# A state-space layer and a linear-attention layer on one core: softplus of dt as one ScalarE table function, first conv taps on ScalarE, and a new order ahead of the scan

## What is computed

```python
xs = clamp(layernorm(groupnorm(x)))                 # 1024 x 256
xin, z = split(xs @ in_proj_w.T)                    # 512 channels each
xc = silu(causal_conv1d(xin, conv_w, 4 taps) + conv_b)
dt, Bm, Cm = split(xc @ x_proj_w.T)                 # 16 + 16 + 16
dt = softplus(dt @ dt_proj_w.T + dt_proj_b)         # 512 channels
h[t] = exp(dt[t] * A) * h[t-1] + dt[t] * xc[t] * B[t]   # 512 x 16 states
y = (h . C + xc * D) * silu(z)
out = clamp(layernorm(clamp(y @ out_proj_w.T)))
```

## Time and profile before

| | us |
|---|---|
| median of 3 runs | 708.2 (707.07 to 708.25) |
| profiled execution, its own time from first to last instruction | 709.2 |
| PE busy | 647.0 (91%) |
| DVE busy | 549.3 (77%) |
| ACT busy | 410.7 (58%) |
| POOL busy | 386.0 (54%) |

### The profile page before, as it was taken

The page is one execution under the profiler, slowest core; times in us unless marked ns, Lnnn a source line. Parts: engine busy times, 40 slices in busy tenths (PEclk is TensorE's granted clock), DMA queues, the critical chain, the costliest instruction groups (busy, mean ns, idle before and its releaser), DMA issues.

```text
span 709.2 us, 25428 instructions
## 1 busy us (share of the span) xinstructions
PE 647.0 (91%) x11476; PEld 450.7 (64%) x11476; DVE 549.3 (77%) x478; ACT 410.7 (58%) x810; POOL 386.0 (54%) x140
## 2 busy tenths in 40 slices
PE   3989986989989999889999999999898999999997
PEld 1434342679978899777898889854345555565532
DVE  5896758488978999799889989863769787892345
ACT  0765789898776777677778767502246346324100
POOL 1000346689996898789889998863101143533000
PEclk9999989999999999999999999999999999999999
DMA  7990352410084201522340100016039899760202
GB/s 213 77 72 4 84 158 114 116 42 18 20 183 90 59 23 24 146 63 63 100 116 18 48 19 18 4 33 184 0 84 199 174 244 228 167 115 2 55 3 119
DMA packets 72627, 62.12 MB, mean 88 GB/s; under 512 B 34024, under 2 KB 57576, under 8 KB 72520
## 3 DMA queue, kind: packets, MB, share of 16 engines
q1 hardware_dynamic: 71560, 60.09, 38.5%
q10 hardware_dynamic: 960, 0.41, 0.2%
HBM read 44.22 MB, written 15.25 MB: 84 GB/s over the span
## 4 chain that ended last, share of the span: by engine, by line
PE 68%; POOL 11%; ACT 9%; DVE 6%; issue 5%; DMA 1%; POOLq 0%; DVEq 0%; ACTq 0%
PE PS L1237 23%; PE PS L1356 8%; PE PS L1470 6%; PE PS L1259 5%; POOL X L572 5%; PE PS L1119 5%; PE PS L1454 4%; POOL arena L572 3%; POOL WIN L572 3%; PE PS L1285 2%; PE PS L1374 2%; PE PS L1256 2%; DVE X L1734 1%; PE PS L1070 1%; PE PS L1335 1%
## 5 line engine op out<-in xcount | busy, mean ns | idle before, releaser
L572 POOL TENSOR_TENSOR X<-X,spare 128x2048 f32<-128x2048 f32 x32 | 146.7, 4584 | 19.2 <-ACT mid L860 9.4
L1237 PE MATMUL PS<-mid,arena 128*32 128x128 f32 x4096 | 138.6, 275 | 9.3 <-issue 8.0
L1237 PEld LDWEIGHTS PS<-mid,arena 128*32 128x32 f32 x4096 | 124.1, 111 | 20.4 <-issue 14.2
L1237 PE MATMUL PS<-WPR,arena 128*32 128x128 f32 x2048 | 130.3, 273 | 4.6 <-issue 1.9
L1237 PE MATMUL PS<-APROD,arena 128*32 128x128 f32 x2048 | 129.5, 273 | 2.9 <-issue 2.9
L1237 PEld LDWEIGHTS PS<-WPR,arena 128*32 128x32 f32 x2048 | 112.1, 110 | 16.0 <-issue 8.9
L1237 PEld LDWEIGHTS PS<-APROD,arena 128*32 128x32 f32 x2048 | 110.7, 110 | 4.7 <-issue 4.1
L852 ACT ACTIVATE arena<-arena,small 128x512 f32<-128x512 f32 (+1 forms) x150 | 99.4, 711 | 22.0 <-DVE X L1734 11.7
L572 POOL TENSOR_TENSOR WIN<-WIN,spare 128x2048 f32<-128x2048 f32 x16 | 73.3, 4584 | 13.3 <-DVE WIN L1734 10.3
L597 POOL TENSOR_TENSOR arena<-arena,PWR 128x512 f32<-128x512 f32 x30 | 42.7, 1450 | 69.3 <-PE PS L1356 69.2
L572 POOL TENSOR_TENSOR arena<-arena,spare 128x2048 f32<-128x2048 f32 x16 | 73.2, 4575 | 9.2 <-DVE arena L1734 5.9
(11 more groups left out here) (203 smaller groups left out, 1192.1 us busy)
## 6 DMA issues: line engine op xcount, KB each, us to landing
arena<-dt_rows SPq DMA_DIRECT2D x56, 256.0 KB, 4.2
arena<-patch_rows SPq DMA_DIRECT2D x40, 324.0 KB, 6.1
patch_rows<-arena SPq DMA_DIRECT2D x10, 648.0 KB, 7.4
X<-in_x SPq DMA_DIRECT2D x4, 1024.0 KB, 7.4
dt_rows<-arena SPq DMA_DIRECT2D x8, 512.0 KB, 2.6
spare<-c_rows SPq DMA_DIRECT2D x64, 64.0 KB, 2.1
tap_rows<-WPR SPq DMA_DIRECT2D x24, 88.0 KB, 8.7
mid<-dt_rows SPq DMA_DIRECT2D x8, 256.0 KB, 3.9
```

Source lines behind the costliest of these rows:

```text
L572: pool.tensor_tensor(HB[s % 4], HB[s % 4], CROW[:, k % 2:k % 2 + 1, :].broadcast_to([P, QN, HALF]), ALU.mult).then_inc(S["g_rd"], 1)
L1237: mm = pe.matmul(PS[32 * n:32 * n + 32, 4 + i, j * P:(j + 1) * P], DXT[:, DT_ * b + g, 4 * h + j, 32 * i:32 * i + 32], DIAGB[k % 2][n][:, ...
```

## The change

Softplus becomes one ACT instruction from PSUM to dt; the passes on DVE and POOL go, and DVE takes the largest dt by a reduction of its own (`largest_dt`). All eight first taps are on ACT. The copies of z pieces 4 and 5 go. The lists of ACT, PE, DVE, POOL and SP and the pairs are written in a new order. The scan no longer waits for corrections (`sp_corr`, `sp_sum`).

```diff
-        PAIR_USERS = ("x3 z0 x6 x7 xd1 V4 V7 tr4 tr6 y0".split(),
-                      "x2 x5 V1 tr0 tr1 V5 tr2 tr3 tr5 tr7 halves0 y1".split(),
-                      "x1 xd0 z1 z2 z3 V3 V6 z7 u0".split(),
-                      "x0 x4 V0 V2 z4 z5 rates0 z6 u1".split())
+        PAIR_USERS = ("z0 x6 V3 z2 z4 z6 V6 tr4 tr6 y0".split(),
+                      "x2 xd0 z1 tr3 rates0 z7 V7 tr5 tr7 halves0 y1".split(),
+                      "x0 x3 x5 V1 tr0 x7 z3 z5 V4 u0".split(),
+                      "x1 x4 V0 V2 tr1 tr2 xd1 V5 u1".split())
-        FIRST_BY_SCALAR = (0, 1, 2)
-        COPIED = (4, 5)
...
@@ SP @@
             first_dt(1)
+            store_dt(2)
+            store_dt(3)
             store_c(1)
-            for e in range(2, NG):
+            for e in range(DT_, NG):
                 store_dt(e)
...
@@ POOL @@
-            def correct(e):
-                pool.wait_ge(S["sp_ln"], e + 1)
-                pool.wait_ge(S["um1_rd"], e + 1)
-                pool.tensor_tensor(LNB[:, e % 2], LNB[:, e % 2], UM1[e % 2], ALU.subtract).then_inc(S["sp_corr"], 1)
...
+            for e in range(NG):
+                times_x(e)
...
@@ ACT @@
-            def positive(e):
+            def softplus(e):
                 act.wait_ge(S["v_ps"], e + 1)
-                act.activation(dt(e), tile_pair("V", e), ACT.Relu).then_inc(S["sp_relu"], 1)
...
+                act.activation(dt(e), tile_pair("V", e), ACT.Softplus).then_inc(S["dt_rd"], 1)
...
-            half_way(4)
-            half_way(5)
+            half_way(0)
             decay(0)
-            take_dxt(3)
+            decay(1)
+            half_way(1)
             take_dxt(4)
+            for e in range(2, 6):
+                half_way(e)
+            take_dxt(5)
+            decay(2)
...
@@ PE @@
             project_in("x", 3)
+            project_in("z", 0)
+            project_in("x", 4)
             pe.wait_ge(S["ld_xp"], 32)
             xdbl(0, 0)
             xdbl(0, 1)
-            project_in("x", 4)
+            xdbl(0, 2)
             project_in("x", 5)
-            xdbl(0, 2)
             xdbl(0, 3)
-            project_in("z", 0)
             b_by_time(0)
+            project_in("x", 6)
             pe.wait_ge(S["ld_dtw"], 64)
             dt_preact(0)
-            project_in("x", 6)
             dt_preact(1)
             project_in("z", 1)
+            dt_preact(2)
+            dx_by_time(0)
+            dt_preact(3)
+            dx_by_time(1)
             project_in("x", 7)
             project_in("z", 2)
-            dt_preact(2)
+            dx_by_time(2)
             project_in("z", 3)
+            dx_by_time(3)
+            project_in("z", 4)
             xdbl(1, 0)
...
+            project_in("z", 5)
+            rates_by_four()
             xdbl(1, 3)
+            project_in("z", 6)
             b_by_time(1)
...
@@ DVE @@
+            def largest_dt(e):
+                dve.wait_ge(S["dt_rd"], e + 1)
+                dve.tensor_reduce(DTMAX[:, e:e + 1], dt(e), mybir.AxisListType.X, ALU.max).then_inc(S["top_rd"], 1)
...
             convolve(6)
-            rounded(0)
...
+            for e in range(DT_):
+                largest_dt(e)
+            rates(0)
             convolve(7)
...
+            for e in range(DT_, NG):
+                largest_dt(e)
             rates(1)
```

More of the change, by code:

```diff
@@ L326, in tile_pair @@
             return pair(pair_of(what, i))
-        def conv_partials(e):
-            return sum(KC - 2 if k in FIRST_BY_SCALAR else KC - 1 for k in range(e))
         def step_of(s):
@@ L694, in silu_gate @@
             def silu_gate(e):
-                if e in COPIED:
-                    act.wait_ge(S["zc_rd"], COPIED.index(e) + 1)
-                    act.activation(SZ[:, e], SZ[:, e], ACT.Silu).then_inc(S["sz_rd"], 1)
-                else:
-                    act.wait_ge(S["zi_ps"], e + 1)
-                    act.activation(SZ[:, e], tile_pair("z", e), ACT.Silu).then_inc(S["sz_rd"], 1)
+                act.wait_ge(S["zi_ps"], e + 1)
+                act.activation(SZ[:, e], tile_pair("z", e), ACT.Silu).then_inc(S["sz_rd"], 1)
             def take_xdbl(b):
@@ L774, in _ @@
             silu_conv(2)
+            silu_gate(0)
+            first_tap(4)
             silu_conv(3)
+            first_tap(5)
             take_xdbl(0)
-            silu_conv(4)
-            silu_gate(0)
             take_bt(0)
+            softplus(0)
+            softplus(1)
+            first_tap(6)
+            softplus(2)
+            take_dxt(0)
+            softplus(3)
+            take_dxt(1)
+            first_tap(7)
             act.wait_ge(S["st_taps"], 16 * QT * 4)
             diagonals(0, 0)
-            positive(0)
@@ L783, in _ @@
-            absolute(0)
+            diagonals(0, 1)
+            silu_conv(4)
+            silu_gate(1)
             silu_conv(5)
-            act.preload_act_table_set(LN_EXP)
-            exponential(0)
-            positive(1)
-            logarithm(0)
-            absolute(1)
-            exponential(1)
-            logarithm(1)
-            silu_gate(1)
             silu_gate(2)
-            positive(2)
+            take_dxt(2)
+            silu_gate(3)
+            take_dxt(3)
             silu_conv(6)
-            absolute(2)
+            silu_gate(4)
@@ L797, in _ @@
             silu_conv(7)
-            silu_gate(3)
-            act.preload_act_table_set(LN_EXP)
-            exponential(2)
-            positive(3)
-            logarithm(2)
-            absolute(3)
-            take_dxt(0)
+            silu_gate(5)
+            take_rates()
+            diagonals(0, 2)
+            diagonals(0, 3)
             take_xdbl(1)
-            exponential(3)
             take_bt(1)
-            logarithm(3)
-            take_dxt(1)
-            positive(4)
-            absolute(4)
@@ L832, in _ @@
-            logarithm(7)
-            diagonals(0, 3)
-            silu_gate(4)
-            take_dxt(2)
-            silu_gate(5)
             silu_gate(6)
             silu_gate(7)
+            softplus(4)
+            softplus(5)
+            softplus(6)
+            softplus(7)
             act.preload_act_table_set(LN_EXP)
@@ L1266, in _ @@
             dx_by_time(4)
+            inputs(0, 1)
             dx_by_time(5)
[L1268 removed]
+            inputs(1, 0)
             dx_by_time(6)
[L1270 removed]
             inputs(1, 1)
@@ L1628, in convolve @@
             def convolve(e):
-                m, own = e % DT_, e not in FIRST_BY_SCALAR
+                m = e % DT_
                 x = tile_pair("x", e)
-                if own:
-                    dve.wait_ge(S["xi_ps"], e + 1)
-                    dve.tensor_scalar(XC[:, e], x, CW[:, m, KC - 1:KC], CB[:, m:m + 1], ALU.mult, ALU.add).then_inc(S["c1_self"], 1)
-                else:
-                    dve.wait_ge(S["c0_rd"], e + 1)
+                dve.wait_ge(S["c0_rd"], e + 1)
                 for k in range(KC - 1):
-                    if k or own:
-                        dve.wait_ge(S["c1_self"], conv_partials(e) + k + own)
+                    if k:
+                        dve.wait_ge(S["c1_self"], (KC - 2) * e + k)
                     part = XC[:, e, KC - 1 - k:]
```

138 lines of the change are left out of this document (17 added, 121 removed).

## The result

| | before | after |
|---|---|---|
| median of 4 runs, us | 707.63 (706.14 to 708.25) | 698.0 (696.97 to 698.69) |
| ratio to before, 95% interval | | 0.9859 (0.9824 to 0.9893) |
| span of the traced execution | 709.2 | 695.9 |
| ACT, DVE, POOL busy | 410.7, 549.3, 386.0 | 392.0, 522.6, 367.1 |
| first, ninth scan | 133.62, 155.82 | 122.43, 147.10 |

The interval is a gain of 7.6 to 12.5 us; forecast were 15.9, and the time lies 0.5 above the forecast's range. At the ninth scan the traces differ by 8.7 us, about what the timed runs give.

The account below looks back on a forecast made before the run. Bound: a relay between engines ahead of the first scan. Walking its steps put that scan 16.6 us earlier, the ninth 22.9 behind it instead of 22.2: gain 15.9, 708.2 - 15.9 = 692.3, range 689.5 to 697.5.

Parts of the forecast that it names:

- Softplus is dear: Rival: a Softplus pass on ACT costs up to 4.08 us instead of 1.02, giving up to 710.7; chance 0.04.
- the prediction's own sign: Forecast is wrong if the scan stage's length from its ninth scan to its end changes by more than a us.
- To 72.6: Walk from 57.6 to 72.6: taps, B transposes about 1.1, x6 projection 3.44, first dt piece at 65.6, then two Softplus.
- the rival's price of 1.6 to 2.5: Rival: PE's clock falls again, one slow stretch costing 1.6 to 2.5 us, 693.9 to 694.8; chance 0.27.
- From the first Softplus to the last gate: Stretch of the walk from 65.6 to 108.0, with PE's projections at 3.44 us each.
- To 117.0: Walk from 108.0 to the first scan at 117.0: last gate, table loads, four Softplus, first decays; DVE's work ends within 0.3.
- The walk puts the ninth scan 22.9 us after the first: Start of the scans: ninth scan 22.9 us after the first, where it was 22.2 before the change.
- The late tiles: Rival: dt tiles for scan steps 2 and 3 land late; two us more of landing cost 1.5, 693.8; chance 0.07.
- the stall: Rival: PE's stall of 3.27 us at 208.92 in the scan stage may fall elsewhere; 689.0 without it; chance 0.05.
- The 0.14 gained at each of three taps: Taps 5, 6 and 7 ahead of the first scan: 1.20 on ACT against 1.34 on DVE, 0.14 gained each.
- nearly three slow stretches: Upper end of the range, 697.5: PE at low clock in nearly three places, which together cost 5.8 us.
- the rival with three slow stretches: Case of the clock rival: all three slow stretches of PE as now, 5.8 us, 698.1; the clock rival's chance 0.27.

Follow-up runs that it names:

- e_full: The changed kernel with 16 unneeded transfers of 256 KB, memory to memory, 8 at a time in steps 8 and 9 of the scan stage: 709.0 us.
- e_pool: The changed kernel with one wait added on POOL: its third product of batch 1 waits for DVE's second `rates` step; 695.93 us.
- e_dx6: The changed kernel with PE's transposes of piece 6 moved ahead of the inputs of step 1, first half: 697.4 us.
- e_loads: The changed kernel with 48 unneeded transfers of 64 KB of dt, 16 in each of steps 7, 8 and 9 of the scan stage: 702.09 us.
- e_taps: The changed kernel with the first taps of pieces 3 to 7 back on DVE: 698.3 us.
- e_best: The changed kernel with the edits of e_x6, e_dx6 and e_pool, and half_way of pieces 6 and 7 ahead of decay 2: 692.88 us.
- e_x6: The changed kernel with PE's x projection of piece 6 moved ahead of the transposes of B of batch 0: 696.95 us.
- e_rates: The changed kernel with the second `rates` step on DVE written in instructions that read one tensor each: 701.72 us.

## Why the prediction was wrong

**What held.** The bound was read rightly: the scans start earlier, the code behind them is the same, and the time followed the ninth scan (8.7 there, 9.6 timed). A Softplus pass of 1.02, the reduction of 1.22 and the loads of 1.28 were right to 0.02, so "Softplus is dear" fell. The removed work was right too: ACT lost 18.7 busy us (24.5 + 1.3 - 6.0 = 19.8 said), POOL 18.9 (19). By the prediction's own sign the scan stage should have kept its length: from the ninth to the last scan it was 310.7 before and 305.4 after. The kernels with one edit or more of the changed one lie between 305.9 and 309.3 (e_full apart), so the sign is too sharp for what single executions do, and whether a part of the 5.3 belongs to the change stays open. The traced execution before was also longer than the prediction took it for, about 2.9 above the median of 708.2 and not 1.0; its sum does not use that.

**Step "To 72.6", 2.7 of the 5.4 at the first scan.** The forecast put the clock at 1.00 behind the rest at 58.2 to 60.1. It fell, at 1.70, inside the rival's price of 1.6 to 2.5, and that rival alone, with 0.27, would have given 694. Another 0.2 is the transposes' later start. The rest of the 2.7 is a term of the sum. From the start of the transposes to the first Softplus I counted 5.5; e_pool, whose clock stayed up, took 6.27. The transposes last 1.53 and not 1.1, and a projection ahead of another step counts its 3.70 to the last result, where I took the spacing of 3.44.

**From the first Softplus to the last gate, 1.0.** PE runs there with hardly a rest, and the same 3.44 stood for each of its projections. That this is the 1.0 is taken from the term above, not shown by a run.

**Step "To 117.0", 1.7: "DVE's last reduction, rates and memset end within 0.3 of that".** This failed outright. I had taken `rates` at its 0.2 without asking what POOL does at that time; the change moves POOL's last four products to just that place. e_pool shows 0.23 with POOL standing, and a first scan 1.6 earlier for it.

**"The walk puts the ninth scan 22.9 us after the first", 1.8.** It was 24.7. The transposes of piece 6 stood behind inputs that wait for the first scan; PE rested 3.24 ahead of them and ran them at a clock of 0.51. e_dx6 takes 3.0 off, more than the walk missed, so the order as such is not the miss; the executions that keep it split the 1.8. In e_loads the clock stayed at 1.00 behind the same rest of 3.24, and the ninth stands 23.6 after the first. In e_taps and e_full the clock fell, but PE did not stall near 136, and it is 23.9. So about 1.1 goes with a second slow stretch and 0.8 with the stall, by single executions. Nor is the gain of e_dx6 safe: e_best has the same order and needs 24.7, behind a tile that came 3.06 late and a stall of 3.68.

**The late tiles and the stall.** Both were in the rivals with small chances, and each as a matter of its own. They hang together: SP's loads fill the queues, ACT waits for the tiles, and PE for its instructions, at 136.41 and 201.06 here and at 208.92 before. In the 3 us ahead of these stalls the DMA share was 1.09, 0.99 and 1.07. It need not be so high: ahead of 275.37 and of a stall of 1.16 at 325.57 it was 0.74 and 0.54.

**The taps.** The 0.14 gained at each of three taps did not show: without the move (e_taps) the time is the same within its interval, and the first scan comes some 0.6 earlier.

**The range.** It ended at 697.5, "nearly three slow stretches" from the forecast. Cases were added one at a time. What came was two slow stretches (1.7 and about 1.1), a wait that no case named (1.7), a stall (0.8) and 2.0 of durations counted short: 7.2 at the ninth scan, 5.7 in the time. That the time missed by less is luck: 0.6 is the kernel before, whose median came out at 707.63 with a fourth run, and 0.9 came back behind the ninth scan. It is luck too that the rival with three slow stretches names 698.1.

## What to carry to other kernels

When a relay is shortened, walk not only the moved steps but what each neighbour does at the new time: a 0.2 us step of DVE beside POOL, a load that fills the queues while PE is due. Filling a rest of PE with another step gave back part of the rest and the clock behind it (2.9 us at the first scan in e_x6), but such a gain reaches the time only when the losses behind it go as well (e_best). Before a large reordering, run the one substitution alone: here it gave most of the gain.

## What the runs showed of the hardware that was not expected

**DVE and POOL.** DVE's instruction on 64 columns took 2.39 us beside POOL's products and 0.23 with POOL standing; in one-input form over SBUF 2.33 on 4 columns. In six traces it ended 0.08 to 0.09 behind one of POOL's products. The reciprocal of 4 columns (0.18) beside the same products did not wait. The reduction over 1024 took 1.21 either way, so not every DVE instruction waits. The Trainium skill, SBUF — State Buffer, SBUF: two separate sides, states that VectorE and GpSimd share a pair of ports under an exclusive lock, which a VectorE instruction with two SBUF inputs or in a two-port mode needs and which is held for a whole instruction. These runs agree: the wait ends with POOL's product, and a second small instruction waits for the next one. Whether the one-input instructions ran in a two-port mode no run shows.

**Full queues and PE.** With a DMA share of 0.9 to 1.07 PE stood up to 4.56 us, and with 0.36 to 0.44 in e_loads not at all. All 83 stalls counted above begin where a block of 256 of PE's instructions ends, and PE goes on 1.2 to 1.7 us after a packet of 16 KB on q8 has landed. The Trainium skill, Runtime: NRT & Kernel Launch, Instruction fetch mechanics, has each engine fetch its instructions in blocks over a queue of its own, mostly hidden. The blocks and the packets of q8 agree with that; beside full queues it was not hidden.

**The clock.** The same rest of 1.39 to 1.40 us, with the same work around it, was followed by a slow stretch with a projection of 5.40 in the changed kernel, e_rates, e_dx6 and e_full (and after 1.31 in e_taps), and by a clock of 1.00 and a projection of 3.70 in e_pool and e_loads. The rest of 3.24 behind the first scan's transposes was followed by 0.51 in the changed kernel and by 1.00 in e_loads. So the first rest was followed by a fall in five executions of seven, and where another step filled it the clock stayed up in five of five. What decides where the rest stands stays open.
